# Attention sums of a two-layer adaLN kernel: all loads after the low parts, and the four reciprocal pieces in one turn

## The reference, cut to what matters

```python
c_q, c_kv = x @ Wq_down, x @ Wkv_down
q_c = (c_q @ Wq_up).reshape(b, s, N_HEADS, HEAD_DIM)      # 128 heads of 4
q_r = (x @ Wq_rope).reshape(b, s, N_HEADS, ROPE)
k_c, v_c = ...                                            # from c_kv
k_r = x @ Wk_rope
scores = (einsum('bqhd,bkhd->bhqk', q_c, k_c) + einsum('bqhd,bkd->bhqk', q_r, k_r)) / scale
attn = softmax(scores, axis=-1)
out = einsum('bhqk,bkhd->bqhd', attn, v_c).reshape(b, s, N_HEADS * HEAD_DIM)
return out @ Wo
```

## Time and profile before

| | |
|---|---|
| median of 3 runs | 2217.44 us (2216.81 to 2218.86) |
| the profiled execution: its time, its span | 2218.86 us, 2216.7 us |
| PE busy | 2156.5 us, 97% of the span |
| DVE busy | 1721.0 us, 78% |
| ACT busy | 1461.9 us, 66% |
| POOL busy | 1215.6 us, 55% |
| mean granted TensorE clock | 0.991 |

### The profile page before, as it was taken

How to read it: one execution, slowest core, us unless ns; L and a number is a source line. 1 busy time by engine, 2 the same in 40 slices (tenths; PEclk the granted TensorE clock), 3 DMA queues, 4 the chain that set the end, 5 groups by cost and what they waited for, 6 DMA issues and landing times.

```text
span 2216.7 us, 41636 instructions
## 1 busy us (share of the span) xinstructions
PE 2156.5 (97%) x11084; PEld 1653.6 (75%) x11084; DVE 1721.0 (78%) x3418; ACT 1461.9 (66%) x2868; POOL 1215.6 (55%) x1086
## 2 busy tenths in 40 slices
PE   7999999999999999999999999999999999999978
PEld 4888888888887657777777777777777777777655
DVE  6777787777777658888888888888888877788755
ACT  3544444444445668888888888888888877777732
POOL 4655656656553446666666666666666621355332
PEclk9999999999999999999999999999999999999998
DMA  7010001001004142111111111111111112333241
GB/s 243 25 43 29 19 28 47 19 28 47 19 0 121 53 174 82 43 48 48 47 47 44 49 47 48 42 48 47 48 44 46 48 48 54 111 113 95 79 130 39
DMA packets 125622, 132.46 MB, mean 60 GB/s; under 512 B 33277, under 2 KB 75805, under 8 KB 125548
## 3 DMA queue, kind: packets, MB, share of 16 engines
q1 hardware_dynamic: 121708, 118.97, 18.1%
q0 software_dynamic: 3840, 12.59, 1.9%
HBM read 101.59 MB, written 29.36 MB: 59 GB/s over the span
## 4 chain that ended last, share of the span: by engine, by line
PE 90%; DVE 5%; issue 2%; DMA 1%; ACT 1%; POOL 1%; SPq 0%; POOLq 0%; DVEq 0%; ACTq 0%
PE bank L2379 12%; PE bank L2386 11%; PE bank L2366 11%; PE bank L1951 9%; PE bank L1953 8%; PE bank L1952 8%; PE bank L2407 6%; PE bank L2298 5%; PE bank L2297 5%; PE bank L2296 5%; PE bank L2404 2%; PE bank L2087 2%; DVE probs L1501 1%; DVE rope_b L1480 1%; DVE rope_a L1478 1%
## 5 line engine op out<-in xcount | busy, mean ns | idle before, releaser
L1761 DVE TENSOR_REDUCE mcol<-bank 128x1 fp32r<-128x512 f32 x1024 | 694.2, 689 | 225.2 <-PE bank L2366 215.3
L2379 PE MATMUL bank<-q,k 128*128 128x512 f32 x1024 | 419.9, 410 | 1.9 <-DMA k<-kc_d 1.9
L2386 PE MATMUL bank<-q,k 128*128 128x512 f32 x1024 | 407.2, 398 | 0.0
L2366 PE MATMUL bank<-km,q 128*128 128x512 f32 x1024 | 404.7, 396 | 2.3 <-DVE mcol L1761 1.1
L2366 PEld LDWEIGHTS bank<-km,q 128*128 128x128 f32 x1024 | 316.2, 309 | 50.3 <-DVE mcol L1761 3.4
L1282 ACT ACTIVATE pT<-bank 128x512 f32<-128x512 f32 x512 | 284.9, 599 | 82.3 <-PE bank L2386 78.4
L1282 ACT ACTIVATE x<-bank 128x512 f32<-128x512 f32 x512 | 284.7, 600 | 81.0 <-PE bank L2386 77.4
L2379 PEld LDWEIGHTS bank<-q,k 128*128 128x128 f32 x1024 | 192.7, 188 | 129.0 <-ACT x L1282 44.3
L2386 PEld LDWEIGHTS bank<-q,k 128*128 128x128 f32 x1024 | 192.8, 188 | 32.5
L2298 PE MATMUL bank<-hT_hi,wr_lo 128*128 128x512 f32 x512 | 203.1, 397 | 0.0
L2296 PE MATMUL bank<-hT_hi,wr_hi 128*128 128x512 f32 x512 | 200.7, 392 | 1.6 <-DVE k L1634 1.6
(11 more groups left out here) (344 smaller groups left out, 5080.0 us busy)
## 6 DMA issues: line engine op xcount, KB each, us to landing
wst<-in_L_attn_Wq_rope SPq DMA_DIRECT2D x64, 256.0 KB, 3.0
o_d<-ost SPq DMA_DIRECT2D x512, 32.0 KB, 1.8
st_q<-in_L_attn_wq SPq DMA_DIRECT2D x8, 1024.0 KB, 7.7
st_wo<-in_L_attn_wo SPq DMA_DIRECT2D x8, 1024.0 KB, 5.2
km<-kc_d SPq DMA_DIRECT2D x256, 32.0 KB
q<-qc_d SPq DMA_DIRECT2D x256, 32.0 KB
k<-kc_d SPq DMA_DIRECT2D x256, 32.0 KB
wm<-in_L_wmod SPq DMA_DIRECT2D x6, 1024.0 KB, 10.0
```

Source lines behind the costliest of these rows:

```text
L1761: dve.tensor_reduce(mcol[:, k % 2, i % 4, i // 4:i // 4 + 1], bank[4 + i % 2][:], AX.X, ALU.max, negate=True)\
L2366: pe.matmul(bank[4 + i % 2][:], q2[:, k % 4, h, i % 4:S:4], km[:, b, h], start=True, stop=True).then_inc(max_mm, 1)
L2379: pe.matmul(bank[s % 4][:], k1[:, k % 2, t], q1[:, k % 4, h], start=True, stop=False)
L2386: pe.matmul(bank[s % 4][:], k2[:, k % 2, h, t], q2[:, k % 4, h], start=False, stop=True).then_inc(scores1, 1)
```

## The change

Three things change; the operations and their number don't.

- POOL issues all eight transfers of a group together, behind a wait for the low part of the group before (`oo_split` at n, where it was n - 1 ahead of the first four), and in even turns behind `split_rope_weights`.
- POOL's `sums_times(n)` and `sums_low(n)` get a step each (1 and 2), and follow `split_rope_weights` in an even turn.
- DVE does the four reciprocal pieces of a group in its step 1, behind reductions 1, 3, 5 and 7. Before, two stood in step 1 (behind 4 and 6) and two in step 2 (behind 1 and 3).

```diff
-SUM_PIECES = ({}, {4: 0, 6: 1}, {1: 2, 3: 3})
-            def load_sums(n, par):
+            def load_sums(n):
                 b, m = n % 2, n // 2
-                if par == 0 and n < B:
+                if n < B:
                     pool.wait_ge(o_stored[b], 64 * (PAIRS - PAIRS // KT))
-                if par == 0:
-                    wait(pool, oo_split, n - 1)
-                    wait(pool, o_added, ADDS * n)
-                for dst, r in zip(SUMS[b], (0, DEN)):
-                    pool.dma_start(dst[:, par], ...).then_inc(parts_loaded, 16)
-                for i in (1, 2):
-                    pool.dma_start(sum_parts[2 * par + i - 1], ...).then_inc(parts_loaded, 16)
+                wait(pool, oo_split, n)
+                for par in range(2):
+                    for dst, r in zip(SUMS[b], (0, DEN)):
+                        pool.dma_start(dst[:, par], ...).then_inc(parts_loaded, 16)
+                    for i in (1, 2):
+                        pool.dma_start(sum_parts[2 * par + i - 1], ...).then_inc(parts_loaded, 16)
...
-            for u in range(HALVED, TAIL + 3 * EARLY + 1):
-                n, step = (u - TAIL) // 3, (u - TAIL) % 3
-                if step == 0 and 0 <= n < EARLY:
-                    load_sums(n, 0)
-                if step == 0 and 0 < n:
-                    sums_low(n - 1)
-                if step == 0 and 0 <= n < EARLY:
-                    load_sums(n, 1)
+            for u in range(HALVED, TAIL + 3 * EARLY):
                 if u % 2 == 0:
                     split_rope_weights((u + 4) // 2, u // 2 % 2)
-                if step == 0 and 0 <= n < EARLY:
-                    sums_add(n)
-                if step == 2 and 0 <= n:
-                    sums_times(n)
+                if u >= TAIL:
+                    n = (u - TAIL) // 3
+                    if (u - TAIL) % 3 == 0:
+                        load_sums(n)
+                        sums_add(n)
+                    elif (u - TAIL) % 3 == 1:
+                        sums_times(n)
+                    else:
+                        sums_low(n)
...
-                        if isinstance(w, int) and w - 2 >= TAIL and i in SUM_PIECES[(w - 2 - TAIL) % 3]:
-                            piece = SUM_PIECES[(w - 2 - TAIL) % 3][i]
-                            sums_reciprocal((w - 2 - TAIL) // 3, slice(piece * S // 4, (piece + 1) * S // 4))
+                        if i in (1, 3, 5, 7):
+                            sums_reciprocal(n, slice((i - 1) * S // 8, (i + 1) * S // 8))
```

More of the change, by code:

```diff
@@ L859, in _ @@
                 turn(u, u % 4, lambda n, u=u: (u + n) // 2)
-            def load_sums(n, par):
+            def load_sums(n):
                 b, m = n % 2, n // 2
-                if par == 0 and n < B:
+                if n < B:
                     pool.wait_ge(o_stored[b], 64 * (PAIRS - PAIRS // KT))
-                if par == 0:
-                    wait(pool, oo_split, n - 1)
-                    wait(pool, o_added, ADDS * n)
-                for dst, r in zip(SUMS[b], (0, DEN)):
-                    pool.dma_start(dst[:, par], o_d[b, 32 * m:32 * m + 32, par, r:r + HD1]).then_inc(parts_loaded, 16)
-                for i in (1, 2):
-                    pool.dma_start(sum_parts[2 * par + i - 1], o_d[b, 32 * m:32 * m + 32, par, i * HD1:i * HD1 + HD1]
-                                   .rearrange("h c (a n) -> h c a n", a=4)).then_inc(parts_loaded, 16)
+                wait(pool, oo_split, n)
+                for par in range(2):
+                    for dst, r in zip(SUMS[b], (0, DEN)):
+                        pool.dma_start(dst[:, par], o_d[b, 32 * m:32 * m + 32, par, r:r + HD1]).then_inc(parts_loaded, 16)
+                    for i in (1, 2):
+                        pool.dma_start(sum_parts[2 * par + i - 1], o_d[b, 32 * m:32 * m + 32, par, i * HD1:i * HD1 + HD1]
+                                       .rearrange("h c (a n) -> h c a n", a=4)).then_inc(parts_loaded, 16)
             def sums_add(n):
@@ L1752, in sums_reciprocal, with maxima @@
                         e.then_inc(o_rden, 1)
-            def maxima(w, k, use, pair, p, quad):
+            def maxima(w, k, use, pair, p, quad, n=-1):
                 if exists(w, UNITS):
@@ L1771, in maxima, with period @@
                     dve.transpose(mrow[:, k % 2].rearrange("p (r i) -> p i r", i=4), mcol[:, k % 2].bitcast(F32)).then_inc(m_turned, 1)
-            def period(u, k, pair, quad):
+            def period(u, k, pair, quad, n=-1):
                 q_low(u + 2, k + 2)
@@ L1779, in period @@
                     split_rope_weights(pair(4), (k // 2) % 2, quad(4))
-                maxima(u + 2, k + 2, pair(2), pair(1), pair(4), quad(4))
+                maxima(u + 2, k + 2, pair(2), pair(1), pair(4), quad(4), n)
                 if not exists(u + 2, UNITS):
@@ L1791, in _ @@
             for u in range(LOOP, UNITS):
-                period(u, u % 4, lambda n, u=u: (u + n) // 2, lambda n, u=u: (u + n) // 4)
+                period(u, u % 4, lambda n, u=u: (u + n) // 2, lambda n, u=u: (u + n) // 4, (u - TAIL) // 3 if (u - TAIL) % 3 == 1 else -1)
             def last_sums(b):
```

## The result

The changed kernel took 2240.34 us in the median of 4 runs (2230.92 to 2243.36), against 2217.12 us (2211.91 to 2218.86, 4 runs) before: ratio 1.0101, 95% interval 1.0067 to 1.0136. Timed again beside the experiments, it took 2237.43 us against 2215.47 (17 runs of before): 1.0102, 1.0085 to 1.0119. So it is some 22 us slower, where 11.4 were forecast and 15.6 was the end of the range.

What follows compares the result with a forecast made beforehand. PE, busy 97%, was taken as the bound, delayed only through DVE. Even groups 3 x (3.3 + 0.1 + 0.2) = 10.8 plus odd 3 x 0.2 = 0.6 gave 11.4 us, so 2217.44 became 2228.8 us; range 2223 to 2233.

Steps and rivals of the forecast that it cites:

- What bounds the kernel, and the road from POOL over DVE to PE: Six-group stretch: PE, busy 97%, bounds; POOL's waits reach PE only through DVE's pieces delaying reductions.
- The only road is DVE: Six-group stretch: a wait of POOL can reach PE only through DVE, since max i waits for reduction i - 2.
- The load of groups 0, 2 and 4: Even turns: eight transfers behind the split take 11.74 us to land, holding DVE 4.5 us and PE 3.3 us.
- as the only row with eight in one go: Even groups' landing time: group 0's 11.74 us from first issue was taken as the basis for all eight transfers.
- Behind it PE goes at its normal pace: Even groups, after PE's stand at max 4: PE runs on normally, with only 0.1 us more for max 6.
- the 0.1 us put on max 6: Even groups: allowance for DVE's piece behind reduction 3 standing in front of reduction 4.
- The term of 3.6 us for an even group: Each even group's cost: 3.3 us stand at max 4, 0.1 for max 6, 0.2 for the pieces.
- Four pieces in one turn: DVE's step 1 in every group: no gap left from reduction 5 on, costing 0.2 us per group, six times.
- The load of groups 1, 3 and 5: Odd turns: eight transfers land at 1939.2, DVE can start at 1940.6, in time by a hair; cost taken as nothing.
- SP's next loads hang on the transposes, which move along with PE: SP's queue: its next loads move along with PE, so the change was put at nothing there.
- the second rival (odd groups late too): Odd loads land 2 us later, DVE 1.9 us late; 2238 us; chance 0.12 shared with dearer pieces.
- What is queued behind POOL's waits: POOL's additions and next split: split about 1 us later in odd groups, PE wants it 3 us or more after; cost nothing.

Runs made afterwards that it cites:

- POOL behind SP's loads: Kernel before, but odd groups' eight transfers wait for the low part and SP's landed km and q, their pieces moved later; ratio 1.0078 to before, 17 us slower.
- DVE held less: Kernel before with the changed piece order and three extra unread reciprocals on DVE ahead of the first piece in groups 0, 2, 4; ratio 1.0019, 4.2 us slower.

## Why the prediction was wrong

- *What bounds the kernel, and the road from POOL over DVE to PE*: right for the even groups. Their waits stand where they were forecast, with the releasers that were forecast. But "The only road is DVE" was wrong: the odd groups' waits of PE come from SP's loads.
- *The load of groups 0, 2 and 4*: right. DVE held 4.62 us (4.5), PE's pause 3.36 (3.3). The load took 11.96 us from first issue to addition; "as the only row with eight in one go" was the right row. The 2.6 us estimated from the Trainium skill's figure (page "DMA: Bandwidth & Descriptors", section "Anatomy of one DMA - SWDGE (gpsimd) path") do not hold for queued transfers here: the last of the eight was landed 7.3 us after its issue (1904.3 to 1911.7), and DVE did wait.
- *"Behind it PE goes at its normal pace"*: this step failed. Behind or just ahead of the pause's end PE was granted half clock in 9 of 12 such turns, for 3.4 us in eight and 6.8 in one. And the 0.1 us put on max 6 was 0.75 where the clock stayed up. The term of 3.6 us for an even group should have been 4.0 at full clock, and it was 4.0 to 6.1 with half clock. In four profiles the three turns together cost 15.1, 11.9, 14.9 and 14.1 us where 10.8 were forecast. Rows of before could have warned: its clock is at 0.81 in the stretch 2104 to 2112 us, behind a wait of PE of 1.94 us for a transfer.
- *Four pieces in one turn, 0.2 us for each group*: too much, if anything. Alone all six together cost 0.2 us in the profile, where 1.2 was taken, and 1.6 us by the times, with an interval that includes nothing.
- *The load of groups 1, 3 and 5, "I take nothing"*: this step failed, and not by its hair. The data came in time for DVE, as worked out. What I didn't look at was whom the eight transfers meet: SP's km and q of the same turn, which PE wants 5 to 7 us after their issue. They cost 4.5, 5.7, 4.7 and 7.5 us in the four profiles of the changed kernel (in the last a pause of 2.47 us in turn 115 had half clock behind it as well), and 3.7 where only the odd groups were late. "SP's next loads hang on the transposes, which move along with PE" looked at when they are issued, not at when they land. Before, half of the bytes went out some 4 us sooner than the rest, all had landed 7.5 to 8.4 us into the turn, and PE didn't wait.
- *The reason against the second rival (odd groups late too)*, "the four-transfer load of group 1 also lay there, and the trace shows no PE wait for it", took half the bytes as evidence for all of them. That rival had the odd groups dear, but by another road (DVE late); its 2238 us came near the measured time by luck.
- *What is queued behind POOL's waits, "3 us or more"*: right for this change (some 5 us in the changed kernel), and what it costs when it is used up was shown with POOL behind SP's loads.

The sum, put together again from the four profiles: even groups 14.0 on average, odd groups 5.6, pieces 0.2, in all 19.8; the stretch grew by 19.6, 17.6, 19.5 and 21.6 us. By the times the kernel is 22 us slower. The 2 to 3 us left stay open. The profiled executions of the changed kernel, 2233.0 to 2237.5 us, are at or below the medians of 2237 to 2240, and above the profiled one of before by only 14 to 19 us, less than their stretches grew: that one, at 2218.86 us, is above its medians of 2214 to 2217. What they fall short goes with the clock elsewhere: outside the stretch PE was at half clock for 39 us in it and for 25, 36, 39 and 18 us in the four of the changed kernel. So the traces don't tell what executions without a profile lose beyond the stretch. Why half clock follows one pause of 3.4 us and not the next stays open too.

## What to carry to other kernels

A transfer that is moved has two prices: when its own reader gets the data, and whose smaller loads it meets on the DMA engines. For the second, list what the other queues issue while the moved transfers are under way, and set the time at which each is read against the time at which the last of the moved ones has landed; evidence from half the bytes is no evidence for all. An in-order engine that everybody waits for should take a late operand behind its urgent work, not in front of it, and where a forecast lets a busy TensorE stand for some 3 us, a stretch at half clock belongs in the sum.

## What the runs showed of the hardware that I had not expected

In the changed kernel pauses of TensorE of 2.45 to 4.01 us at max 4, amid full work, went with half clock in 9 of 12 turns. Eight of these had it for 3.4 us and were longer than 10.41 us by the pause and another 1.4 to 1.5 us; one had it for 6.8 us, with 2.4 us on top of the pause; the three at full clock had 0.65 to 0.67 on top. The half clock began between 1.2 us before work was taken up again and 1.6 us after. Over all profiles here, 16 of 20 pauses of 3 to 4 us from turn 107 to 123 went with it. Shorter ones did so more seldom: PE's wait of 2.3 to 2.6 us in turn 126 was followed by it in 6 of 14 profiles, and the three pauses of 1.6 us with DVE held less were not, their turns being 1.5 us longer.

Eight transfers of 256 KB from POOL, where half of them had gone out some 4 us sooner before, took the landing time of SP's 32 KB stores issued right behind from 2.2 to 4.5 us. The Trainium skill's page "DMA: Bandwidth & Descriptors", section "Queues, rings and completion order", says that a DMA engine takes turns between the queues that it has work for, packet by packet. The trace agrees as far as it can be read: SP's first store, issued at 1937.20 when seven of POOL's eight had been issued whole, landed 4.5 to 5.2 us later, so by 1942.4, before POOL's last transfer at 1943.0; it was slowed and not held until POOL's had gone. The packets' order is in no trace.
